# A three-layer graph network: a new division of the row fetches among four engines

## The reference

```
def _rgcn_layer(x, src, dst, edge_type, W, W_root, b):
    out = x @ W_root + b
    x_src = x[src]
    for r in range(R):
        mask = (edge_type == r).astype(x.dtype)
        agg = segment_sum(x_src * mask[:, None], dst, num_segments=n)
        cnt = segment_sum(mask, dst, num_segments=n)
        out = out + (agg / maximum(cnt, 1.0)[:, None]) @ W[r]
    return out
```

## Time and profile before

| | us |
|---|---|
| median of the runs | 3166.51 |
| the profiled execution | 3171.93 |
| its span, first to last instruction | 3170.1 |

### The profile page before, as it was taken

One profiled execution on the slowest core, in us unless ns is written; L12 is line 12 of the kernel. 1 busy time (PEld: TensorE's weight loads), 2 busy tenths in 40 slices (PEclk: granted clock), 3 DMA queues, 4 the chain that ended last, 5 costly groups with the idle time before them and its releaser, 6 DMA issues. The chain is left out here.

```text
span 3170.1 us, 85791 instructions
## 1 busy us (share of the span) xinstructions
PE 2080.0 (66%) x13052; PEld 1904.3 (60%) x13052; DVE 1498.6 (47%) x7818; ACT 995.7 (31%) x5111; POOL 2285.6 (72%) x2413
## 2 busy tenths in 40 slices
PE   7977777777777566555665665656656655655666
PEld 6866666666666555555655555545555655555556
DVE  5545444545444344445444444434444444444444
ACT  1132222222222243333333333224333333333323
POOL 6647777777777477777777777747777777777773
PEclk6578888988887687787677777778777777788778
DMA  3112222222222322222222222222222222222222
GB/s 104 49 34 56 56 56 56 56 56 56 55 56 55 83 55 55 55 55 55 55 55 55 55 55 55 55 83 55 56 55 55 55 55 55 55 55 55 55 80 80
DMA packets 119471, 185.19 MB, mean 58 GB/s; under 512 B 46075, under 2 KB 77482, under 8 KB 118922
## 3 DMA queue, kind: packets, MB, share of 16 engines
q0 software_dynamic: 76736, 157.31, 19.1%
q1 hardware_dynamic: 40026, 21.85, 2.5%
q10 hardware_dynamic: 2160, 0.56, 0.1%
HBM read 169.93 MB, written 9.60 MB: 57 GB/s over the span
## 5 line engine op out<-in xcount | busy, mean ns | idle before, releaser
L478 POOL DMA_INDIRECT ring<-node_table,src_t x1588 | 1506.7, 949 | 539.7 <-issue 387.4
L1265 PE MATMUL ps_a<-onehot,ring 128*128 128x128 f32 x4992 | 889.0, 333 | 946.2 <-DMA ring<-node_table,src_t 709.0
L1265 PEld LDWEIGHTS ps_a<-onehot,ring 128*128 128x128 f32 x4992 | 764.6, 234 | 1023.0 <-DMA ring<-node_table,src_t 710.2
L688 DVE TENSOR_SCALAR onehot<-iota,key,weight 128x128 f32<-128x128 f32 x2496 | 880.6, 365 | 940.2 <-DVEq L302 934.0
L478 POOL DMA_INDIRECT ring<-in_x,src_t x810 | 776.4, 959 | 299.0 <-issue 187.5
L1275 PE MATMUL ps_o<-sums,w_rel 128*128 128x128 f32 x4992 | 908.2, 359 | 61.1 <-PEq L302 61.1
L1275 PEld LDWEIGHTS ps_o<-sums,w_rel 128*128 128x128 f32 x4992 | 888.5, 276 | 70.1 <-issue 70.0
L993 ACT COPY sums<-ps_a 128x512 f32<-128x512 f32 x624 | 365.7, 586 | 1713.7 <-ACTq L302 1651.8
L964 ACT COPY act_cols<-h_t 128x1 f32 x4096 | 435.7, 187 | 118.9 <-issue 92.9
L699 DVE TENSOR_TENSOR out_t<-out_t,ps_o 128x16 f32 x2496 | 434.6, 174 | 56.0 <-DVEq L302 41.6
L712 DVE COPY dve_cols<-h_t 128x1 f32 x2048 | 245.5, 154 | 198.9 <-DVE out_t L699 102.3
(11 more groups left out here) (148 smaller groups left out, 503.0 us busy)
## 6 DMA issues: line engine op xcount, KB each, us to landing
ring<-node_table SPq DMA_DIRECT2D x3584, 0.5 KB
ring<-in_x SPq DMA_DIRECT2D x1792, 0.5 KB
ring<-node_table,src_t POOLq DMA_INDIRECT x1588
ring<-in_x ACTq DMA_DIRECT2D x1024, 0.5 KB
ring<-in_x,src_t POOLq DMA_INDIRECT x810
node_table<-ring SPq DMA_DIRECT2D x24, 256.0 KB
out_rows<-ring SPq DMA_DIRECT2D x12, 256.0 KB
w_rel<-in_L_gnn_Ws SPq DMA_DIRECT2D x3, 512.0 KB, 4.1
```

What stands on the lines that cost most here:

```text
L478: nc.gpsimd.indirect_dma_start(out=ring[:, q % G, t, :], out_offset=None, in_=source, in_offset=bass.IndirectOffsetOnAxis(ap=src_t[:, q * ...
L688: ins = nc.vector.tensor_scalar(onehot[:, b, t, :], iota_1[:, :], key[:, col:col + 1], weight[:, col:col + 1], ALU.is_equal, ALU.mult)
L1265: ins = nc.tensor.matmul(ps_a[b][:, t * KEYS:(t + 1) * KEYS], ring[:, q % G, t, :], onehot[:, b, t, :], start=True, stop=True)
```

## The change

`COLUMNS` gives the slots from one column tile to the next (0: none in layer one). `SYNC_TILES` becomes a pair, one number for layer one and one for the others. The table of layer one comes out as before. In layers two and three it changes as follows:

| tiles of a layer | before | after |
|---|---|---|
| ScalarE's columns | 16, every 12 slots | 33, every 6 slots |
| VectorE's columns | 8, every 24 slots | 12, every 16 slots |
| SyncE's rows | 14, slots 20 to 202 | 13, slots 16 to 194 |
| GpSimd's gathers | 794 | 774 |

```
-SYNC_TILES = 14
+SYNC_TILES = (14, 13)
-COLUMNS = {"act": (GT - 2, (0, 12)), "dve": (GT - 3, (0, 24))}
+COLUMNS = {"act": (GT - 2, (0, 6)), "dve": (GT - 3, (0, 16))}
...
-    at = spread(20, NQ - 6, SYNC_TILES) if kind else [14, 24] + spread(G + 2, NQ - 10, SYNC_TILES - 2)
+    at = spread(16, NQ - 14, SYNC_TILES[1]) if kind else [14, 24] + spread(G + 2, NQ - 10, SYNC_TILES[0] - 2)
```

## The result

The kernel takes 3117.16 us in the median of 20 runs, against 3166.18 us for 20 runs of the kernel before: a ratio of 0.9846, 95% interval 0.9838 to 0.9853, or 49.0 us less. Two of the 20 runs lie far off, at 3159.43 and 4866.98 us, and are left out of the ratio; no trace of them was kept. The profiled execution took 3117.26 us with a span of 3115.4. The forecast was 3116.4 us, from 3109 to 3127.

What follows compares the result with a forecast made beforehand. GpSimd's count of gathers was taken to bound layers two and three; 20 fewer in each at 1.2536 us save 50.1 us, other engines' added work hidden. 3171.93 becomes 3121.8 us profiled, 3116.4 us median, range 3109 to 3127.

Steps and rivals of the forecast that it cites:

- What bounds: Layers two and three: GpSimd's count of gathers sets their length, 794 each at 1.2536 us, 4.787 us a slot.
- What the change removes: GpSimd in layers two and three: 20 gathers each, 25.07 us a layer, 50.1 us in all.
- the signs: Signs of being right: 774 gathers at 1.253 to 1.255 us, lasting 970 us, layer gap 28 us, TensorE and ScalarE still waiting.
- ScalarE hidden: ScalarE's 17 added tiles a layer: 23.8 us per six slots against GpSimd's 28.0, 85% loaded, so hidden.
- a tile's extras: ScalarE's per-tile cost beyond copy groups: first-group delay 0.4, landing copy 0.27, row-number issues 0.49 and 0.2 us.
- the step on ring slots: ScalarE: single slots of 4.2 us or more do no harm, as evacuations hand ring slots back 26 slots ahead.
- The rival of ScalarE: ScalarE becomes the bound, still waiting 1.10 us a slot for TensorE: 3284 us median; decides from 28.0 us per six slots; 4%.
- VectorE hidden: VectorE's 4 added tiles a layer: a one-group slot takes 3.53 us, 76% of 4.665, so hidden.
- VectorE's copies against GpSimd: Whether added VectorE copies slow GpSimd: 0 taken, upper end 61.4 us a layer; as rival 3239 us median, 2%.
- SyncE: SyncE's 13 earlier tiles land before GpSimd fills their slots: margins 10.8, 8.7 and 27 us, so no cost.
- The rival's price: SyncE late at 72 us a tile, 13 slots at about 4 us following: time 3166 us, little or no gain; 3%.
- this bound: TensorE's load: at the lower clock level 95% of the new slot plus 0.7% for tiles; hidden, but closest of all.

Runs made afterwards that it cites:

- the last run of all: Changed kernel with a VectorE column tile every 12 slots and SyncE's 14 tiles as before, 769 gathers a layer: 3106.49 us, ratio 0.9809 to the kernel before.

## Why the prediction was right, point by point

- **What bounds.** Right. Over all runs in which no other engine took over, the time follows GpSimd's count: 790, 777, 774, 773, 770, 769 and 734 gathers gave 8.0, 41.9, 49.0, 51.0, 60.3, 59.5 and 146.6 us less, where 1.2536 us each gives 10.0, 42.6, 50.1, 52.7, 60.2, 62.7 and 150.4.
- **What the change removes.** 20 gathers a layer, 50.1 us forecast, 49.0 measured. That is closer than the runs can tell: the ratio's interval is 46.5 to 51.3 us. A layer's gathers: 970.3 forecast, 969.2 and 969.4. Two of the signs came out just beside what was named: 1.2523 us per gather for 1.253 to 1.255, and a gap between the layers of 26.6 us for 28.
- **ScalarE hidden.** Right, with less room than I had. The term that was mis-sized is a tile's extras: 1.4 us in the sum, 2.1 to 2.3 measured with every 5 slots. Six slots are then up to 22.4 + 2.3 = 24.7 us of 28.0, 88% and not 85%. ScalarE's timeline in the changed kernel shows one tile's period, from landing to landing:

```profile
1525.17 0.27 ACT L970 COPY ring<-ps_w 128x128 f32<-128x128 f32 x1
...
1529.26 0.59 ACT L993 COPY sums<-ps_a 128x512 f32<-128x512 f32 x1
...
1533.53 0.59 ACT L993 COPY sums<-ps_a 128x512 f32<-128x512 f32 x1
...
1536.96 0.59 ACT L993 COPY sums<-ps_a 128x512 f32<-128x512 f32 x1 [0.61 <-ACTq L302]
...
1542.08 0.59 ACT L993 COPY sums<-ps_a 128x512 f32<-128x512 f32 x1 [0.32 <-ACTq L302]
...
1546.34 0.59 ACT L993 COPY sums<-ps_a 128x512 f32<-128x512 f32 x1
...
1551.89 0.59 ACT L993 COPY sums<-ps_a 128x512 f32<-128x512 f32 x1 [2.46 <-ACTq L302]
1552.37 0.27 ACT L970 COPY ring<-ps_w 128x128 f32<-128x128 f32 x1
```

  27.2 us, with three-group slots of 4.27 us (1529.26 to 1533.53), and 2.46 us of waiting in one place before the period closes. Half the evacuations follow the copies at once, and it harms nothing, as the step on ring slots had it; so what the prediction named as a sign against it, evacuations that follow copies at once, is none by itself.
- **The rival of ScalarE.** It did not come about, and nothing speaks against its point of decision: "no more gain beyond 28.7" is 4.787 us a slot. At some 4.1 (every 6 slots) there was the full gain, at 4.85 to 4.89 (every 5 slots) the kernel was 12 us slower than before. The mechanism that I gave it, the 1.10 us wait for TensorE after each slot's copies, did not appear there; the copies and the tile's extras alone filled the time.
- **VectorE hidden.** Right in the outcome, its load mis-sized: 3.53 us was one of two kinds of slot, and the changed kernel shows both in a row.

```profile
1514.19 0.35 DVE L688 TENSOR_SCALAR onehot<-iota,key,weight 128x128 f32<-128x128 f32 x1 [0.38 <-DVEq L302]
1516.67 0.96 DVE L712 COPY dve_cols<-h_t 128x1 f32 x8 [0.86 <-DVE out_t L699]
1518.21 0.35 DVE L688 TENSOR_SCALAR onehot<-iota,key,weight 128x128 f32<-128x128 f32 x1 [0.58 <-DVEq L302]
1520.41 0.95 DVE L712 COPY dve_cols<-h_t 128x1 f32 x8 [0.57 <-issue]
1521.74 0.34 DVE L688 TENSOR_SCALAR onehot<-iota,key,weight 128x128 f32<-128x128 f32 x1 [0.38 <-DVEq L302]
```

  4.02 us, then 3.53. The mean of 3.78 is 81% of 4.66, not 76%.
- **VectorE's copies against GpSimd.** Zero taken, and zero found with the copies doubled.
- **SyncE.** Right. Its first two tiles were issued by 1175.76 and 1243.14 (timeline below), and GpSimd's gathers for slots 16 and 30 end at 1103.66 + 66 x 1.2522 = 1186.3 and at 1251.4: margins of 10.5 and 8.3 us, where I had 10.8 and 8.7. With 14 tiles the margin was to shrink, and it did wherever ScalarE's part was in: in layer two TensorE waited for SyncE's rows 3.7 us with that part alone, 15.0 with both parts and 28.1 with VectorE every 12 slots. But none of these runs was slower by an amount that shows, so the thirteenth tile was not what made the change safe. The rival's price had slots of 4 us behind the last late tile; they took 2.6 us with 40 gathers left out and 2.6 to 3.2 in the last run of all, and the lag was made up.

```profile
1109.51 66.25 SPq L409 DMA_DIRECT2D ring<-node_table  x128
...
1177.32 65.82 SPq L409 DMA_DIRECT2D ring<-node_table  x128
```

- **TensorE.** It waits for gathers as forecast (341.8 us, "some 300"). What the lower clock level does to this bound stays open: one of the 20 runs, at a mean granted clock of 0.65 where most had 0.78 to 0.81, took 3131.86 us, 15 us above the median, and no trace of it was kept.

## What to carry to other kernels

Where one engine runs without a pause and the others wait for it, the worth of taking work off it is its count times its pitch (the time from the start of one piece of work to the next), read from its own timeline. The price for the engines that receive the work has to be read where they run back to back, over a whole period and all kinds of slots: one cheap slot (3.53 for a mean of 3.78) stood behind a next step that by its price was to gain 17.5 us on the change and lost 66, and the small extras of a tile (1.4 for 2.3 us) behind one that was to be even and lost 60. And with a deep ring between them, an overloaded consumer does not show as a stall of the producer, as long as the ring can hold its lag, but as a longer time behind the producer's last piece of work in a stage.

## What had not been expected

- The next step is a cliff, not a slope: VectorE every 12 slots gains some 12 us on the change, every 10 loses some 66; ScalarE every 6 gains, every 5 loses some 60.
- SyncE late by up to 12.7 us cost nothing that shows, with slots of 2.6 us behind the last column copies.
- The gather's pitch itself differs a little between the profiled executions, from 1.2500 to 1.2539 us in a layer, where GpSimd did not wait. From 1.2536 before to 1.2523 after makes 2.0 us over both layers, of the 4.6 us between the span's 54.7 and the forecast's 50.1. What it comes from stays open.
